# Row-sum reciprocals by DMA and a three-operation leaky activation on GpSimd in a graph-attention head loop

## The reference, cut to what matters

```
def gat_layer(x, graph, W, b):
    h = x @ W
    s = einsum('bnd,bmd->bnm', h, h) * graph
    s = where(s == 0.0, NEG_INF, s)
    a = softmax(s, axis=2)
    return einsum('bnm,bmd->bnd', a, h) + b
heads = vmap(lambda W, b: gat_layer(flow_x, graph, W, b))(Wh, bh)
cat   = moveaxis(heads, 0, 2).reshape(B, N, H * D)
x     = leaky_relu(cat, negative_slope=0.01)
out   = gat_layer(x, graph, W_out, b_out)
return leaky_relu(out, negative_slope=0.01)
```

## Time and profile before

| | |
|---|---|
| median of 3 runs | 3390.68 us (3390.52 to 3391.51) |
| the profiled execution | 3389.07 us, its span 3387.3 us |
| busy share of the span | PE 91%, PEld 56%, DVE 88%, ACT 68%, POOL 25% |
| the head loop's weigh operations | 350.1 to 2123.3 us in the span |

### The profile page before, as it was taken

The page is one execution under the profiler, slowest core; times in us unless marked ns, Lnnn a source line. Parts: engine busy times, 40 slices in busy tenths (PEclk is TensorE's granted clock), DMA queues, the critical chain, the costliest instruction groups (busy, mean ns, idle before and its releaser), DMA issues. The chain is left out here.

```text
span 3387.3 us, 48344 instructions
## 1 busy us (share of the span) xinstructions
PE 3089.4 (91%) x15547; PEld 1885.1 (56%) x15547; DVE 2982.4 (88%) x3851; ACT 2300.4 (68%) x3525; POOL 830.0 (25%) x580
## 2 busy tenths in 40 slices
PE   7998899999999999999999999799598888888857
PEld 3676566666666666666666666599554333333323
DVE  3578999999999999999999999688756999999944
ACT  0122677777777777777777777677346999999831
POOL 0123000000000000000000000000114999999921
PEclk9999999999999999999999999899799999999978
DMA  4000000000000000000000000000000000000001
GB/s 97 0 1 1 1 1 0 0 0 0 0 0 0 0 0 0 0 0 0 0 0 0 0 0 0 1 1 0 9 0 1 1 1 1 1 1 1 1 2 25
DMA packets 30364, 12.16 MB, mean 4 GB/s; under 512 B 27984, under 2 KB 29264, under 8 KB 30288
## 3 DMA queue, kind: packets, MB, share of 16 engines
q1 hardware_dynamic: 25056, 10.04, 1.3%
q10 hardware_dynamic: 5232, 1.12, 0.2%
HBM read 9.06 MB, written 2.10 MB: 3 GB/s over the span
## 5 line engine op out<-in xcount | busy, mean ns | idle before, releaser
L660 ACT ACTIVATE hid_work<-hid_work,hid_nmax 128x1024 f32<-128x1024 f32 x512 | 589.5, 1151 | 305.5 <-DVE hid_nmax L644 305.5
L632 DVE TENSOR_TENSOR hid_work<-hid_score_ps,A 128x1024 f32<-128x1024 f32 x512 | 618.3, 1208 | 30.0 <-PE hid_score_ps L593 29.9
L644 DVE CUSTOM_DVE_ANT_0 hid_work<-hid_masks,hid_work 128x1024 f32<-128x1024 f32 x512 | 620.6, 1212 | 0.2 <-DVE hid_masks L652 0.2
L1690 POOL TENSOR_TENSOR el<-el,node_edge 128x1024 f32<-128x1024 f32 x256 | 610.5, 2385 | 17.8 <-DVE el L1672 11.5
L671 ACT COPY hid_probsT<-hid_turn_ps 128x512 f32<-128x512 f32 x1024 | 542.2, 580 | 101.9 <-PE hid_turn_ps L607 101.9
L607 PEld LDWEIGHTS hid_turn_ps<-ident,hid_work 128*128 128x128 f32 x4096 | 458.4, 141 | 249.3 <-issue 206.0
L607 PE MATMUL hid_turn_ps<-ident,hid_work 128*128 128x128 f32 x4096 | 544.9, 276 | 4.9 <-ACT hid_probsT L671 3.9
L818 PE MATMUL hid_mix_ps<-hid_probsT,x_now 128*64 128x512 f32 x2048 | 497.2, 606 | 33.4 <-DVE hid_Zn L892 30.5
L592 PE MATMUL hid_score_ps<-hid_SX,hid_Y 128*128 (+1 forms) x1024 | 476.9, 466 | 2.6 <-DVE hid_SX L993 2.6
L593 PE MATMUL hid_score_ps<-hid_SX,hid_Yl 128*128 (+1 forms) x1024 | 405.5, 396 | 0.0
L1643 PE MATMUL spread<-hT_parts,pick 128*128 128x512 f32 x1024 | 309.2, 425 | 65.9 <-DVE u_buf L1666 61.6
(11 more groups left out here) (280 smaller groups left out, 4080.2 us busy)
## 6 DMA issues: line engine op xcount, KB each, us to landing
A<-in_adj_dram SPq DMA_DIRECT2D x4, 1024.0 KB, 9.8
X<-in_x_dram SPq DMA_DIRECT2D x8, 256.0 KB, 8.8
out_dram<-X SPq DMA_DIRECT2D x8, 256.0 KB, 3.4
wa<-in_L_gnn_weight_dram ACTq DMA_DIRECT2D x2, 256.0 KB, 15.2
wb<-in_L_gnn_weight_dram ACTq DMA_DIRECT2D x2, 256.0 KB, 13.6
wh<-in_L_gnn_Wh_dram SPq DMA_DIRECT2D x2, 256.0 KB, 5.5
incid<-in_L_gnn_H_dram SPq DMA_DIRECT2D x2, 256.0 KB, 3.5
wo<-in_L_gnn_W_out_dram SPq DMA_DIRECT2D x1, 256.0 KB, 6.1
```

The source lines that it names most:

```text
L632: nc.vector.tensor_tensor(work[:, kk % 4, :], score_ps[kk % 2][:], A[:, kk % NT, :], ALU.mult).then_inc(s["weighted"], 1)
L644: nc.vector.tensor_tensor_reduce(work[:, kk % 4, :], masks[:, kk % 2, :], work[:, kk % 4, :], -1.0, 3.0e38, ALU.add, ALU.min, nmax[:, kk % ...
L660: nc.scalar.activation(work[:, kk % 4, :], work[:, kk % 4, :], ACT.Exp, bias=nmax[:, kk % 4:kk % 4 + 1], scale=-1.0, accum_out=rowsum[:, k ...
L1690: nc.gpsimd.tensor_tensor(el[:, q % ELS, :], el[:, q % ELS, :], coefT[:, q // C, :], ALU.mult).then_inc(s_weighted, 1)
```

## The change

Two things change in the head loop.

The reciprocals no longer pass through TensorE and ScalarE. SyncE waits for VectorE's reciprocal, stores the 128 x 4 numbers to a DRAM tensor `r_rows` with the tile index outside and the partition inside (one element of 4 bytes at a time), waits for this transfer, and loads the 512 numbers back as one row broadcast to all 128 partitions (256 KB into `rbc`), then waits for that too before the next group. Norm waits for `r_loaded` in place of `misc_read`; the early table loses its R entries.

The leaky operation leaves VectorE. GpSimd does it in three operations on 128x512: `sloped` = 0.01 v; v = max(v, 0) * 0.99 in place; v = v + `sloped`. Each waits for the one before by a semaphore. They stand in GpSimd's program among the stagings.

One line outside the loop only drops a semaphore that nothing uses.

```diff
-            EARLY = {0: ("R", 8), 2: ("W", 14), 4: ("R", 8), 6: ("W", 14), 8: ("R", 8), 10: ("W", 14), 12: ("R", 8),
-                     14: ("W", 14)}
+            EARLY = {2: ("W", 14), 6: ("W", 14), 10: ("W", 14), 14: ("W", 14)}
...
-                if EARLY[k][0] == "R":
-                    pe.wait_ge(s["inverted"], g + 1)
-                    pe.nop(nofuse=True)
-                    for a in range(GROUP):
-                        slot = u * NT + half * GROUP + a
-                        done = nc.tensor.transpose(misc_ps[:, a * P:(a + 1) * P],
-                                                   at.rinv[:, slot:slot + 1].to_broadcast([P, P]), ident[:])
...
-                    nc.scalar.copy(rbc[:], misc_ps[:]).then_inc(misc_read, 1)
...
-            def vec_leaky(vec, i, k, first, last):
-
-                if not present(k, False, first, last) or EARLY[k][0] != "W":
-                    return
+            def pool_leaky(pool, i, k, first=False, last=False):
+
                 _, u, half, _ = group_of(i, k, EARLY[k][1])
                 part = leaky[:, u, half, :]
-                vec.wait_ge(misc_read, use(i, k, False, first, last) + 1)
-                nc.vector.scalar_tensor_tensor(out=part, in0=part, scalar=0.01, in1=part, op0=ALU.mult,
-                                               op1=ALU.max).then_inc(leaky_made, 1)
+                n = 0 if first else 4 * i - 3 + k // 4
+                if not first:
+                    pool.wait_ge(leaky_made, n)
+                    pool.nop(nofuse=True)
+                pool.wait_ge(misc_read, use(i, k, False, first, last) + 1)
+                pool.nop(nofuse=True)
+                nc.gpsimd.tensor_scalar(sloped[:], part, SLOPE, None, ALU.mult).then_inc(leak_parted, 1)
+                pool.wait_ge(leak_parted, 2 * n + 1)
+                pool.nop(nofuse=True)
+                nc.gpsimd.tensor_scalar(part, part, 0.0, 1.0 - SLOPE, ALU.max, ALU.mult).then_inc(leak_parted, 1)
+                pool.wait_ge(leak_parted, 2 * n + 2)
+                pool.nop(nofuse=True)
+                nc.gpsimd.tensor_tensor(part, part, sloped[:], ALU.add).then_inc(leaky_made, 1)
...
-                vec.wait_ge(misc_read, use(i, k - 2, False, first, last) + 1)
+                vec.wait_ge(r_loaded, 64 * i + 16 * ((k - 10) // GROUP + 1))
...
+            def sp_body(sp, i, first=False):
+
+                for d in range(4):
+                    sp.wait_ge(s["inverted"], 4 * i + d + 1)
+                    sp.nop(nofuse=True)
+                    sp.dma_start(r_rows[d].rearrange("a q -> q a"), at.rinv[:, d * GROUP:(d + 1) * GROUP],
+                                 allow_slow_non_contiguous=True).then_inc(r_stored, 16)
+                    if not first or d >= 1:
+                        sp.wait_ge(s["normed"], 4 * i + d)
+                        sp.nop(nofuse=True)
+                    sp.wait_ge(r_stored, 64 * i + 16 * (d + 1))
+                    sp.nop(nofuse=True)
+                    sp.dma_start(rbc[:], r_rows[d].rearrange("a q -> (a q)").unsqueeze(0).to_broadcast([P, HALF])
+                                 ).then_inc(r_loaded, 16)
+                    sp.wait_ge(r_loaded, 64 * i + 16 * (d + 1))
+                    sp.nop(nofuse=True)
```

More of the change, by code:

```diff
@@ L545, in adjacency_stack_kernel @@
         MASKED = -1.0e16
+        SLOPE = 0.01
         BODY = 2 * NT
@@ L765, in pe_early @@
                 g, u, half, ib = group_of(i, k, EARLY[k][1])
-                if EARLY[k][0] == "R":
-                    pe.wait_ge(s["inverted"], g + 1)
-                    pe.nop(nofuse=True)
-                    for a in range(GROUP):
-                        slot = u * NT + half * GROUP + a
-                        done = nc.tensor.transpose(misc_ps[:, a * P:(a + 1) * P],
-                                                   at.rinv[:, slot:slot + 1].to_broadcast([P, P]), ident[:])
[L773 to L778, removed]
+                if u == 0 and half == 0:
+                    pe.wait_ge(staged_w, ib + 1)
+                pe.wait_ge(s["normed"], g + 1)
+                pe.nop(nofuse=True)
+                done = nc.tensor.matmul(misc_ps[:], wh_now[:], Zn[:, half, :], start=True, stop=True)
                 done.then_inc(misc_made, 1)
@@ L830, in act_early @@
                 act.wait_ge(misc_made, n + 1)
[L831 to L834, removed]
-                    nc.scalar.copy(rbc[:], misc_ps[:]).then_inc(misc_read, 1)
-                else:
-                    nc.scalar.activation(leaky[:, u, half, :], misc_ps[:], ACT.Identity,
-                                         bias=bh_now[:]).then_inc(misc_read, 1)
+                nc.scalar.activation(leaky[:, u, half, :], misc_ps[:], ACT.Identity,
+                                     bias=bh_now[:]).then_inc(misc_read, 1)
             def act_late(act, i, k, first, last):
@@ L881, in vec_invert @@
                 vec.wait_ge(s["exped"], GROUP * (g + 1))
+                if not first:
+                    vec.wait_ge(r_stored, 64 * i + 16 * ((k - 6) // GROUP) - 32)
+                    vec.nop(nofuse=True)
                 nc.vector.reciprocal(at.rinv[:, slots], at.rowsum[:, slots]).then_inc(s["inverted"], 1)
@@ L910, in vec_step @@
                 vec_norm(vec, i, k, first, last)
-                if k:
-                    vec_leaky(vec, i, k - 1, first, last)
                 at.vec_shift(vec, i, k, first, last)
@@ L952, in pool_body @@
                 stage_x(pool, bass.ds((i + 1) // HEADS % J, 1), 0)
+                pool_leaky(pool, i, 14, first)
                 if not first:
@@ L962, in adjacency_stack_kernel, with _ @@
             block = scope.enter_context(nc.Block())
+            @block.sync
+            def _(sp):
+                sp_body(sp, 0, first=True)
+                with sp.Fori(1, ITEMS) as i:
+                    sp_body(sp, i)
             @block.gpsimd
@@ L971, in _ @@
                     pool_body(pool, i)
+                for k in (2, 6, 10):
+                    pool_leaky(pool, ITEMS, k, last=True)
             @block.scalar
```

11 lines of the change are left out of this document (9 added, 2 removed).

## The result

The changed kernel takes **3756.88 us** (median of 4 runs, 3752.60 to 3762.35) beside 3391.10 us for the kernel before on the same chip (3390.52 to 3391.82): ratio 1.1084, 95% interval 1.1069 to 1.1099. It is 366 us slower, 11.8 us an item, where 16 us in all were forecast, and lies outside the range. The profiled execution has a span of 3760.5 us.

What follows compares the result with a forecast made beforehand. The path alternates between TensorE (12.56 us) and VectorE (43.06 us), 55.62 us an item. Removals give 53.38, held operations add 2.75, transfers nothing: 56.13 us, 16 us more over 31 periods, 3407 us forecast, range 3352 to 3465 us.

Steps and rivals of the forecast that it cites:

- the triples: GpSimd's three leaky operations per group, holding VectorE's shift and mask: 2.75 us lost an item.
- The size of the store: Store of the reciprocals to DRAM: 3.5 us, high end 5.7 from a load of 1024 4-byte elements.
- transfers at nothing: Store, load and hand-overs between reciprocal and norm: 7.5 us, hidden with 2 us to spare, adding nothing.
- The load: Broadcast load of the row into `rbc`: 3.5 us from issue to landing, from the 256 KB row.
- The time at hand, 9.7 us,: Shortest stretch available to the transfers, from the reciprocal of step 14 to the norm of step 2: 9.7 us.
- the rival of late transfers: Norm waits for the load, holding VectorE's queue and TensorE's burst: about 155 us slower, 3545 us, chance 0.04.
- R at 0.44 us: Turned reciprocals on TensorE, step 8's lying on the path: removing them saves 0.44 us an item.
- The price of GpSimd's tensor_scalars: First two of GpSimd's leaky operations: 0.61 us each, as a copy; all three with hand-overs 2.81 us.
- The rival: GpSimd's tensor_scalars cost more than a copy: 0.95 us gives 3458 us, 1.29 us gives 3529 us; chance 0.18.
- the prediction's sign: In the changed kernel's profile, GpSimd's first operation taking over 0.8 us would show dearer tensor_scalars.
- That every GpSimd operation holds shift and mask for its whole length: VectorE's shift and mask lose GpSimd's end minus their own start minus 0.13 us; weigh and norm free.
- the sum: Head-loop period: 53.38 us plus 2.75 us of losses, 56.13 us an item, over 31 periods giving 3407 us.

Runs made afterwards that it cites:

- The triples alone: Kernel before with only the leaky operation moved to GpSimd's three operations, reciprocals still through TensorE and ScalarE: 3387.49 us in 11 runs, ratio 0.9994.
- 64 bytes apart: Changed kernel with leaky on VectorE, 512 elements stored 64 bytes apart into a second tensor, a constant row loaded: 3372.96 us.
- the spaced forms: Changed kernel with leaky on VectorE, elements stored 64, 32 or 16 bytes apart, constant row loaded: 3372.96, 3374.28 and 3376.30 us.
- free transfers: Changed kernel without transfers or turned reciprocals, norm multiplying by a constant written once, leaky in three operations on GpSimd: 3416.87 us, ratio 1.0078.

## Why the prediction was wrong

The sign was forecast right, by luck: slower because of the triples. The triples alone change nothing (0.9994); the kernel is slower because of the transfers, which had 4 in 100.

- **The size of the store** is the step that failed. "I take 3.5 us for each" put store, load and hand-overs at 7.5 us, high end 11.9; measured from reciprocal to norm they take 12.9 to 14.4 us, 13.5 in the mean (14.21 from 1227.03 to 1241.24), of which 8.7 pass from the store's issue to the load's. The 5.7 us row loads 1024 elements of 4 bytes, and it was called a high end although a store had no row at all. It was no bound: this store of 512 packed elements takes 8.7 us. With 2 us to spare on a sum of two unknown terms, "transfers at nothing" was worth far more doubt than 4 in 100.
- **The load** was a smaller miss: 4.7 us for 3.5.
- **The time at hand, 9.7 us,** was right: where norm does not wait (64 bytes apart) the shortest stretch from reciprocal to norm is 10.44 us, with leaky's 0.60 still in it. Spaced elements need 2.5 + 3.1 us and hand-overs and fit; the packed ones go past it, and then all that the rival of late transfers describes happens: norm waits, shift, mask and weigh stand behind it, TensorE behind them. That rival gave 3545 us with 11.9 us; with 13.5 its own rule has waits of 3.8 and three times 2.8, less 0.8, 11.4 us an item, against 11.8 measured. That is nearer than the rule deserves, since it has no term for what lengthens the stretch from norm to reciprocal by 0.44 us. The mechanism was named, its price was not.
- **R at 0.44 us** holds: an item takes 55.65 us in the trace of the kernel before and 55.22 to 55.23 in the spaced forms.
- **The price of GpSimd's tensor_scalars** was wrong: 0.61 us, taken from a copy, against 1.50 and 1.93. The triple takes 5.0 us, not 2.81. The rival had 0.95 and 1.29; by the prediction's sign (a first operation of over 0.8 us) it holds, yet its 3458 and 3529 us are far above the 3416.87 measured with free transfers, for the reason in the next point. The Trainium skill's "GPSIMD Engine Reference" (Engine selection) has one-input operations at roughly line rate; the copy's 0.61 us agrees, the tensor_scalars do not, and the measurement decides.
- **That every GpSimd operation holds shift and mask for its whole length** was wrong for tensor_scalars and right for two-input operations, whose loss it gives to 0.01 us. The rule of the Trainium skill's "SBUF — State Buffer" (Who interferes with whom), that whoever comes first keeps the other out for a whole instruction, is borne out here by the two-input operations alone. The rows that I argued from the earlier trace rows were all of such operations.
- **The drain** had no term. The prediction counts 31 periods; behind them every kernel with the triple takes 9 to 12 us longer than its like with leaky on VectorE where no transfer is late; for 8.8 us of these TensorE waits for the last two triples (12.1 for 3.3).
- With free transfers the sum says 3407 us, and 3416.87 is measured: 56.28 us an item for 56.13, and the drain. It is near for partly wrong reasons, since the errors in the price and in the hindrance work against each other.
- **TensorE's clock** was in no term. In the change it is granted 0.94 in the loop in place of 1.00, and the burst means 699 ns in place of 606. By the starts of norm at most 6 us of this lie on the path.

## What to carry to other kernels

A row of single 4-byte elements gathered from 128 partitions into packed DRAM was slow to complete here, with 512 bytes as with 2 KB; 16 bytes of each partition in one run, or spaced elements, were quick. Price a store by a store, never by a load. Where two transfers in a row must fit between two steps of a loop, compute the loop's new period with each at twice its estimate before putting them at nothing. Work moved to GpSimd costs more by where its two-input operations fall than by how long it runs: look for the VectorE operation beside them, and let them wait for it. And look at the ends of a loop, where nothing covers the longer work.

## What was not expected of the hardware

- The packets of a 2 KB store were moved within 1 us, and its completion came 9 us later (8.7 us from its issue to the load's in the mean); 512 elements 64 bytes apart complete in 2.5 us.
- GpSimd: 1.50 us for multiply and 1.93 us for maximum and multiply over 128x512 f32, one input each, against 0.61 us for a copy and 1.26 to 1.29 us for a two-input operation undisturbed.
- After 4.27 us without work TensorE's granted clock was at the 1.2 GHz level, and the next burst took 3.68 us in place of 1.94.
- A norm that reads one input in steps of 4 elements takes 1.06 us in place of 0.68.
